# A transformer chain on one core: the router's steps in the rope jobs at other positions, two rope projections in another PSUM bank, four sums at position 21

## The reference

```
x = x + attn_a(layernorm(x))   # 4 layers: 16-head attention with alibi and causal mask, then
                               # a GELU feed-forward of 512; a layer norm at the end
x = x + moe(layernorm(x))      # router: project to a ball, hyperbolic distance to 8 centroids,
                               # the 2 nearest experts, softmax weights; 8 experts of 512
x = x + attn_b(layernorm(x))   # one attention with rotary positions (rope), 16 heads of 8
x = x + moe(layernorm(x))      # the same experts and router again
```

## Time and profile before

| | us |
|---|---|
| median of 3 runs (lowest, highest) | 2834.51 (2833.81, 2839.74) |
| the profiled execution | 2838.04 |
| its span, first to last instruction | 2836.3 |
| rope slots 0 to 7, from the first Exp of the first to the last of the eighth | 478.5 of the span |
| one Exp of ACT, mean | 0.599 |
| one Max of DVE, mean (0.6 apart when back to back) | 0.685 |
| one scatter or gather call on POOL, mean | 1.0 |

### The profile page before, as it was taken

The page is one execution under the profiler, slowest core; times in us unless marked ns, Lnnn a source line. Parts: engine busy times, 40 slices in busy tenths (PEclk is TensorE's granted clock), DMA queues, the critical chain, the costliest instruction groups (busy, mean ns, idle before and its releaser), DMA issues.

```text
span 2836.3 us, 52348 instructions
## 1 busy us (share of the span) xinstructions
PE 2449.8 (86%) x19582; PEld 1526.6 (54%) x19582; DVE 1864.4 (66%) x5205; ACT 1467.7 (52%) x2646; POOL 911.5 (32%) x1038
## 2 busy tenths in 40 slices
PE   3799999999999999999999998896878888879964
PEld 2355555554555555545555554586754444547854
DVE  6877777777777777777778885332567777753112
ACT  0356666666666666666665655433234444454421
POOL 6233233333332333333323433231412332322144
PEclk9799999999999999999999999998989899999987
DMA  4252233233323332332312220456721221105754
GB/s 108 74 156 92 96 99 117 79 101 107 95 94 99 95 121 79 99 110 86 98 59 63 80 67 15 132 161 174 212 81 55 67 65 59 59 13 171 211 162 117
DMA packets 158013, 285.56 MB, mean 101 GB/s; under 512 B 22264, under 2 KB 111992, under 8 KB 156024
## 3 DMA queue, kind: packets, MB, share of 16 engines
q1 hardware_dynamic: 149376, 264.23, 30.7%
q0 software_dynamic: 8384, 17.97, 2.1%
HBM read 227.33 MB, written 95.96 MB: 114 GB/s over the span
## 4 chain that ended last, share of the span: by engine, by line
PE 52%; DVE 22%; ACT 12%; issue 5%; POOL 4%; another core or an unknown queue 3%; SPq 1%; DMA 1%; POOLq 0%; ACTq 0%; DVEq 0%
PE bank L589 9%; DVE mx L1215 8%; PE bank L551 7%; PE bank L567 6%; ACT big L816 4%; PE bank L725 4%; PE bank L661 4%; PE bank L735 4%; PE bank L650 4%; PE bank L553 2%; PE bank L517 2%; PE bank L609 2%; POOL big L1509 1%; ACT fhT L847 1%
## 5 line engine op out<-in xcount | busy, mean ns | idle before, releaser
L816 ACT ACTIVATE big<-bank 128x512 f32<-128x512 f32 x1600 | 932.1, 599 | 890.2 <-PE bank L567 496.8
L1215 DVE TENSOR_REDUCE mx<-bank 128x4 f32<-128x512 f32 x1600 | 1049.3, 685 | 421.3 <-PE bank L553 406.4
L551 PE MATMUL bank<-KS,QS 96*128 96x512 bf16 (+3 forms) x2560 | 694.9, 312 | 101.8 <-DVE mx L1215 67.0
L567 PE MATMUL bank<-QS,KS 99*128 99x512 bf16 (+3 forms) x2560 | 629.3, 308 | 34.4 <-ACT big L816 23.7
L1509 POOL TENSOR_SCALAR_AFFINE_SELECT big<-big 128x768 f32<-128x768 f32 (+1 forms) x416 | 265.3, 661 | 770.7 <-ACT big L816 770.7
L553 PE MATMUL bank<-mask_a,ident_b 128*128 128x128 bf16 x2560 | 496.3, 225 | 0.0
L551 PEld LDWEIGHTS bank<-KS,QS 96*128 96x128 bf16 x2560 | 257.4, 101 | 414.4 <-DVE mx L1215 210.6
L589 PE MATMUL bank<-big,V 128*9 128x512 f32 (+3 forms) x5120 | 434.2, 444 | 16.6 <-POOL big L1509 10.8
L567 PEld LDWEIGHTS bank<-QS,KS 99*128 99x128 bf16 x2560 | 215.5, 100 | 165.6 <-ACT big L816 82.6
L884 ACT ACTIVATE big<-bank,big 128x256 f32<-128x256 f32 x368 | 150.8, 471 | 277.7 <-PE bank L725 195.3
L553 PEld LDWEIGHTS bank<-mask_a,ident_b 128*128 128x128 bf16 x2560 | 258.8, 101 | 55.7 <-issue 32.0
(11 more groups left out here) (216 smaller groups left out, 2917.2 us busy)
## 6 DMA issues: line engine op xcount, KB each, us to landing
big<-e_pack SPq DMA_DIRECT2D x92, 578.0 KB
QS<-part_scr SPq DMA_DIRECT2D x480, 96.0 KB
KS<-part_scr SPq DMA_DIRECT2D x480, 96.0 KB
part_scr<-parts SPq DMA_DIRECT2D x80, 384.0 KB
x_rows<-in_alibi SPq DMA_DIRECT2D x47, 384.0 KB, 4.9
y_rows<-in_alibi SPq DMA_DIRECT2D x47, 384.0 KB, 5.5
big<-x_rows SPq DMA_DIRECT2D x92, 128.0 KB
y_rows<-big SPq DMA_DIRECT2D x92, 128.0 KB
```

The source lines that it names most:

```text
L551: mm(bk[:, col:col + w], Q[0:ROW_MAX, hh, t * P:(t + 1) * P], K[0:ROW_MAX, hh, 0:w], start=True, stop=False)
L567: last = mm(bk[:, col:col + w], K[0:ROWS, hh, t * P:(t + 1) * P], Q[0:ROWS, hh, t * P:T], start=(n == 0 or b + j < CLEARED), stop=(b + j < ...
L816: A(dst, src, ACT.Exp).then_inc(exp_done, 1)
L1215: v.tensor_reduce(dst, src, axis=AX.X, op=ALU.max).then_inc(a_used, 1)
```

## The change

Three edits, all in the rope jobs. The second and fourth of the four rope projections of jobs 2 to 7 go to the bank of the value products; the second waits until that bank has been copied out, the third and the fourth until the bank they write was read two projections before, and the value products of a job wait for the rotation of the job two ahead. The router's steps take other positions. The sums of streams 4 to 7 go from position 15 to 21, and the gathers of streams 5 to 7 to 22, 26, 30, 34.

```diff
+SPREAD_ROPE = (8, 10, 12, 15, 17, 20, 23, 26)          # SPREAD = (6, 9, 11, 14, 16, 18, 22, 25)
...
+        def bank_of(j, k):
+            return bankPV if j >= 2 and k % 2 else bankF
...
-        COMBINE = {1: (-2, 27), 2: (-1, 8), 3: (-1, 28), 4: (1, 15), 5: (2, 15), 6: (3, 15), 7: (4, 15)}
-        GATHER = {1: (-2, 15, 1), 2: (-2, 36, 1), 3: (-1, 16, 1), 4: (0, 16, 5), 5: (1, 18, 5), 6: (2, 18, 5), 7: (3, 18, 5)}
+        COMBINE = {1: (-2, 27), 2: (-1, 8), 3: (-1, 28), 4: (1, 21), 5: (2, 21), 6: (3, 21), 7: (4, 21)}
+        GATHER = {1: (-2, 15, 1), 2: (-2, 36, 1), 3: (-1, 16, 1), 4: (0, 16, 5), 5: (1, 22, 4), 6: (2, 22, 4), 7: (3, 22, 4)}
...  project_rope(b, j, k), PE
                     if k == 0:
                         pe.wait_ge(xnT_ready, XT_B + j + 1)
+                    elif j < 2:
+                        pe.wait_ge(rproj_used, ROPE_EACH * j + k)
+                    elif k == 1:
+                        pe.wait_ge(ot_done, QUADS * (b + j - 2))
                     else:
-                        pe.wait_ge(rproj_used, ROPE_EACH * j + k)
-                    mm(bankF[:], bp_sb[:, k * D:(k + 1) * D], xnT[:], start=True, stop=True).then_inc(rproj_ready, 1)
+                        pe.wait_ge(rproj_used, ROPE_EACH * j + k - 1)
+                    mm(bank_of(j, k)[:], bp_sb[:, k * D:(k + 1) * D], xnT[:], start=True, stop=True).then_inc(rproj_ready, 1)
...  pv(b, j, g, tiles_of_keys), PE, at g == 0
                             pe.wait_ge(v_ready, b + j + 1)
+                            if rope_job and j + 2 < JOBS:
+                                pe.wait_ge(rproj_used, ROPE_EACH * (j + 3))
...  PE
-                    route = ((route_transposes, -1, 22), (route_project, -1, 23), (route_dots, -1, 25), (route_ranks, -2, 3))
+                    route = ((route_transposes, -1, 24), (route_project, -1, 27), (route_dots, -1, 30), (route_ranks, -2, 4))
...  ACT
-                    route = ((route_columns, 22), (route_squares, 24))
+                    route = ((route_columns, 24), (route_squares, 28))
...  DVE (rotate reads bank_of(j, n) in place of bankF)
-                    route = ((route_layernorm, -1, 19), (route_apply, -1, 21), (distances, -1, 26), (distances_2, -1, 27),
-                             (distances_3, -1, 28), (nearest, -1, 31), (nearest_2, -1, 32), (picked, -1, 35),
-                             (places, -2, 4), (weights, -2, 16))
+                    route = ((route_layernorm, -1, 19), (route_apply, -1, 21), (distances, -1, 31), (distances_2, -1, 34),
+                             (distances_3, -1, 36), (nearest, -1, 38), (nearest_2, -2, 0), (picked, -2, 1),
+                             (places, -2, 6), (weights, -2, 18))
...  POOL
-                    route = ((lambda S: route_rsqrt(JOBS + S), -1, 20), (norm_root, -1, 26), (picked_root, -1, 37)) + tuple(
-                        (lambda S, c=c: scatter(S, (c,)), -2, at) for c, at in enumerate(SPREAD))
+                    route = ((lambda S: route_rsqrt(JOBS + S), -1, 20), (norm_root, -1, 32), (picked_root, -2, 3)) + tuple(
+                        (lambda S, c=c: scatter(S, (c,)), -2, at) for c, at in enumerate(SPREAD_ROPE))
```

More of the change, by code:

```diff
@@ L1182, in rotate @@
                             dve.wait_ge(p3_ready, 2 * (b + j))
-                        v.tensor_tensor(qk[:, k, :], bankF[:], rope_sb[:, 2 * k, :], ALU.mult).then_inc(rproj_used, 1)
+                        v.tensor_tensor(qk[:, k, :], bank_of(j, n)[:], rope_sb[:, 2 * k, :], ALU.mult).then_inc(rproj_used, 1)
                     else:
-                        v.tensor_tensor(rtmp[:, k, :], bankF[:], rope_sb[:, 2 * k + 1, :],
+                        v.tensor_tensor(rtmp[:, k, :], bank_of(j, n)[:], rope_sb[:, 2 * k + 1, :],
                                         ALU.mult).then_inc(rproj_used, 1)
```

## The result

The kernel before has a median of 2837.06 us beside the changed one's 2828.99 us (20 runs each, 2829.60 to 2847.19 and 2818.39 to 2840.89): ratio 0.9971, 95% interval 0.9961 to 0.9981. The change makes the kernel faster by 8 us (5.4 to 11). Forecast were 29 us and a median between 2789 and 2826, so the sign is right and the size is not. The execution profiled after took 2828.95 us, 9.1 less than that of before.

What follows compares the result with a forecast made beforehand. No engine fills a rope slot; order of work and waits set the time. Gains and losses summed to 31.9 us, less 3 for clock, rounded to 29: 2834.5 - 29 = 2805.5 us median, range 2789 to 2826.

Steps and rivals of the forecast that it cites:

- the wait at 7: OT transposes at position 7 wait 1.6 us for places; +1.0 us for positions 3 to 12 in slots 2 to 5.
- Positions 22 to 30, gain 42.3: Router waits of slots 1 to 5 hidden under chunks, leaving 12.4 us (11.9 in slot 5); gains sum to 42.3 us.
- Gather calls behind it on GpSimd: Six gathers and two scatters after the combine, before position 32's root: claimed hidden by under 2 us.
- Positions 31 to 39, -11.1: Router steps moved here onto VectorE: +2.4 us in each of slots 1 to 4, +1.5 in slot 5.
- Positions 0 to 2, -2.4: VectorE gets 2.5 us more work here, nearly all hidden: +0.6 us in each of slots 2 to 5.
- Bank: Third and fourth rope projections lose their waits, 1.07 us a slot; 0.6 and 0.7 booked in slots 0 and 1.
- Combine at 21, -4.0: Combine meets layer norm and apply in positions 19 to 25: +1.0 us in each of slots 1 to 4.
- Slot 6, 6.7 - 0.3: Positions 22 to 30 gain 1.2 us, the maxima's split wait 5.5; positions 3 to 12 cost +0.3.
- Clock, -3: Kept TensorE-bound positions 22 to 30: a fifth at half rate, about 6 us, partly counted already, so -3 us.
- The work is only moved: Rival, chance 0.14: VectorE is the real bound, positions 31 to 12 grow; 10 to 15 us remain, 2820 to 2824.
- The clock comes back: Rival, chance 0.13: spread waits keep full clock in slots 1 to 5; 12 to 15 us beyond forecast, 2791 to 2793.
- The slower rival: Chance 0.07: the wait for places at position 7 costs over 7.3 us in each of five slots; 2838 to 2845 us.

Runs made afterwards that it cites:

- e15: The kernel before, unchanged, as a control on a 2755 chip: median 2754.25 us, ratio 0.9987 to before.
- e12: The changed kernel, unchanged, on a 2755 chip: median 2729.86 us, ratio 0.9912 to before.
- e8: Changed kernel with the gathers of streams 5 to 7 as plain row copies without indices, 2838 chip: median 2806.49 us, ratio 0.9879 to before.
- e7: Changed kernel with ranks back at position 3 and places at 4, 2838 chip: median 2812.70 us, ratio 0.9912 to before.
- e2: Kernel before with only the bank of the second and fourth rope projection changed, 2755 chip: median 2745.79 us, ratio 0.9965 to before.
- e3: Kernel before with only the combine and gathers at their new positions, 2755 chip: median 2746.66 us, ratio 0.9960 to before.
- e4: Changed kernel with combine and gathers put back to their old positions, 2755 chip: median 2733.97 us, ratio 0.9916 to before.
- e5: The kernel before, unchanged, run again on a 2838 chip: median 2838.32 us, ratio 1.0001 to before.
- e6: The changed kernel, unchanged, run again on a 2838 chip: median 2827.96 us, ratio 0.9956 to before.
- e18: Changed kernel with ranks at 3, places at 4, combine and gathers at old positions, 2838 chip: median 2804.43 us, ratio 0.9919 to before.
- e17: Changed kernel with ranks at 3, places at 4, gathers five positions apart from 22, 2838 chip: median 2795.23 us, ratio 0.9891 to before.
- e9: Changed kernel with ranks at 3, places at 4, combine and gathers at old positions, 2755 chip: median 2719.23 us, ratio 0.9848 to before.

## Why the prediction was off, step by step

The sum failed in two of its steps, and the first carries most of it (18.2 us of some 31; the wait at 7 and VectorE's work in positions 31 to 2 carry 10.7).

*Positions 22 to 30, gain 42.3; with the combine's -4.0 in them and 19 to 21, 38.3.* The failed step is "Gather calls behind it on GpSimd ... Hidden, by under 2 us" together with the 12.4 us kept in slots 1 to 3. Measured on the chip of the profile: 20.1 us over positions 19 to 30 of slots 1 to 5. On the 2755 chip (e15 to e12), where nothing starts late, the same stretch gains 40.6, so what the step had wrong is the price of the gather calls and nothing else in it. Slots 4 and 5 keep 13.9 and 14.1; slots 1 to 3 keep 19.0, 22.7 and 23.0 in place of 12.4. e8 brings these to 13.7, 14.1 and 13.9, and e12 has 12.9, 13.9 and 14.0 on another chip. I priced the calls by when GpSimd would be free and not by what happens to the others while it issues them. The trace of before held the warning: beside its calls ScalarE stands 4.19 us, with "remote" as the releaser, slots 2 and 3 have 3 us more than slot 1 in positions 19 to 21, and slot 0, with eight gather calls in a row and no router, takes 11.3 us for these three positions.

```profile
2238.04 0.60 ACT L816 ACTIVATE big<-bank 128x512 f32<-128x512 f32 x1 [4.19 <-remote]
```

*The wait at position 7, worked out at 1.6 us and booked at +1.0 a slot.* It measured 2.71 us, and positions 3 to 12 of slots 2 to 5 grew by 8.5 us in sum, not 4.0 (11.3 on the 2755 chip). The mechanism and its place were right; the size lacked the 0.95 us of one shut-out instruction and the lower clock behind the wait. e7 shows both: 2.5 to 5.3 us back in each slot. My bound of +2.5 held for slots 3 and 4 (+1.3 each) and not for 2 and 5 (+3.0, +2.9).

*Positions 31 to 39, -11.1.* Measured -13.0 (+2.2 to +3.0 a slot, and 2.9 in slot 5 against 1.5); -7.5 on the 2755 chip. About right.

*Positions 0 to 2, -2.4.* Measured -6.7, 1.1 to 2.4 a slot in place of 0.6 (-7.3 on the 2755 chip). In slot 2 VectorE is busy 4.96 of 5.30 us, just the 2.5 + 2.5 that I had. The busy time was right and the conclusion wrong: 4.96 us of VectorE leave no room in 4.3 + 0.6. Why slot 3 takes 6.6 is open; e12 has 6.6 there too, so it isn't the kind of chip.

*Bank.* The third and fourth projection wait for nothing, as forecast; +2.5 in slots 0 and 1 against 1.3, and e2 shows 1.2 us a slot elsewhere against 1.07. Right.

*Combine out of 13 to 18, +1.6*: 0.9 in slots 1 to 4. *Combine at 21, -4.0*: wrong in sign where it stands alone. Slots 1 to 4 average 62.7 us in e3 and 65.5 in e15, two 2755 chips; in slot 2 positions 13 to 18 take 9.0 and not 9.6, 19 to 21 take 2.9 and not 3.6, 22 to 25 take 10.1 and not 11.5. Under the router's waits the combine at 21 was free, by one profile of each. Beside the router's new steps it gave nothing more: e4 without it has 0.9916, e12 with it 0.9912.

*Slot 6, 6.7 - 0.3*: measured 7.6. The 5.10 us before the maxima's transposes are gone; they follow directly:

```profile
2508.47 0.54 PE L646 MATMUL bank<-ident_b,mparts 128*128 128x128 bf16 x4
```

*Slot 7, +1.8*: -0.2, and -1.3 on the 2755 chip: positions 22 to 30 kept 12.1 us (5.0 + 7.1). Wrong, small.

*Clock, -3.* Positions 22 to 30 stand at 1.00 in slot 4 (0.72 before), and in e12, without holds, in each of slots 1 to 5: the clock came back with the waits gone. Slot 2 goes from 0.87 to 0.88 only, its holds and the wait at 7 keeping it down.

*The rivals.* "The work is only moved" came nearest by its gain (10 to 15 us, measured 8) and only in part by its mechanism: positions 31 to 12 took 28.2 us more where 17.5 were booked (11.1 + 2.4 + 4.0), so 10.7 us of the shortfall are VectorE's and the places', and 18.2 (38.3 - 20.1) stand in positions 19 to 30, from a hold that is not VectorE. "The clock comes back" happened in its positions and gave nothing beyond the forecast's. The slower rival was the wait at 7, which needed 7.3 us a slot and had about 2. On the 2755 chip positions 3 to 12 and 0 to 2 cost even more (11.3 and 7.3 where 4.0 and 2.4 were booked), and the eight slots still gained 26.6 of the 31.9.

What stays open: how indirect calls on GpSimd hold TensorE's semaphore updates up, and whether TensorE itself is late with them (its ends are modelled), why only on some chips, and which share belongs to the call and which to its transfer. The first profile's 0.8 us for the eight slots against 4.3 in e5 and e6 is the spread between executions, which I can't divide further. And slot 1, with gathers alone, has no long hold at the old positions (e18, rows of two, four and two calls, latest reader 1.9 us late) but one of 3.6 us in e17 behind a row of four: the length of the row isn't all of it.

## What to carry to other kernels

A wait that is taken away must be checked for what it covered: look for late starts with "remote" as the releaser near DMA-issuing GpSimd calls, price these as if they were in the open, and count how many of the calls the new order puts in a row. When VectorE's small steps are moved, look at GpSimd's operation beside their new place, not at VectorE's queue alone. A kernel that runs on several chips should be tried on both kinds: here one edit was worth 8 to 10 us on one and 25 on the other, while two numbers for ranks and places were worth 15 on both (e6 to e7 by the medians; e4 to e9 by the eight slots, each on its own chip).

## What of the hardware was not expected

- The same program takes 2755 us on three chips and 2827 to 2838 on two. The first 31 encoder jobs take the same (1742.5 against 1740.5 us in the kernel before). The difference stands behind them: over all kernels the last encoder job with the first round of tiles takes 325 to 330 against 342 to 353 us, the tail 227 to 232 against 261 to 269, and the rope slots of the kernel before 461.7 against 478.5.
- Beside indirect DMA calls on GpSimd, 0.97 us each and 1.3 us apart, TensorE's semaphore updates came so long after the modelled ends of its products on the 2838 chips that idle readers started up to 6.2 us late, 5 to 9 us a slot. In the rope slots no single call did it (0 of 64), and every row of six to eight did (29 of 29). On the 2755 chips there was none. With plain copies in the gathers' place no reader was over 0.8 us late in slots 1 to 3.
- A VectorE product over 32 columns took 1.14 us beside a GpSimd subtraction over 512, in place of 0.19, in all of four slots.
